# Squares, output weights and first feed-forward weights on GpSimd, and a linear layer inside the second mix

## What is computed

```python
x = _layernorm(x + L0_attn(x))   # differential attention, 16 heads of two score maps, full
x = _layernorm(x + L0_ffn(x))    # integer weights 2048 x 512, silu(g) * u
x = _layernorm(x + L1_attn(x))   # differential attention, causal, grouped keys and values
x = _layernorm(x + L1_ffn(x))    # x @ (weight * scale[:, None]).T + bias
# in both attentions, with attn1, attn2 = softmax(q k^T / 4) v of the two halves of a head:
attn = attn1 - lambda_full * attn2                             # 32 values a head
attn = attn * rsqrt(mean(attn * attn, -1) + 1e-5) * subln_w * (1.0 - LAMBDA_INIT)
out = attn.reshape(b, t, 512) @ wo.T
```

## Time and profile before

| | |
|---|---|
| three runs, us | 2482.46, 2478.36, 2482.72 (median 2482.46) |
| the profiled execution | 2479.18 us, span 2477.4 us |
| PE busy | 2344.1 us (95% of the span) |
| DVE busy | 1678.0 us (68%) |
| ACT busy | 1252.5 us (51%) |
| POOL busy | 190.1 us (8%) |
| phases, us from the start | L0 attention to 1021.2, mix0 to 1107.5, feed-forward to 1678.5, L1 attention to 2326.1, mix1 to 2412.7, linear to 2477.4 |

### The profile page before, as it was taken

The page is one execution under the profiler, slowest core; times in us unless marked ns, Lnnn a source line. Parts: engine busy times, 40 slices in busy tenths (PEclk is TensorE's granted clock), DMA queues, the critical chain, the costliest instruction groups (busy, mean ns, idle before and its releaser), DMA issues. The chain is left out here.

```text
span 2477.4 us, 43796 instructions
## 1 busy us (share of the span) xinstructions
PE 2344.1 (95%) x15600; PEld 1331.8 (54%) x15600; DVE 1678.0 (68%) x3848; ACT 1252.5 (51%) x2467; POOL 190.1 (8%) x341
## 2 busy tenths in 40 slices
PE   6999999999999999879999999967999999999877
PEld 5663333333333333458888888856644444444456
DVE  2357888888888887583344434452488888888586
ACT  2126666667666666652221121232266666666653
POOL 3000000000000000100000000000012211221103
PEclk9999999999999999999999999988899999999998
DMA  5664222232122200000000000003622222210001
GB/s 192 165 137 85 57 27 27 33 45 30 27 27 28 27 1 2 31 30 22 26 26 25 25 25 25 1 0 105 142 41 41 41 41 41 40 23 3 27 1 68
DMA packets 56684, 109.09 MB, mean 44 GB/s; under 512 B 11820, under 2 KB 22060, under 8 KB 56488
## 3 DMA queue, kind: packets, MB, share of 16 engines
q1 hardware_dynamic: 53960, 96.84, 19.7%
q0 software_dynamic: 2528, 9.70, 1.1%
HBM read 73.75 MB, written 31.46 MB: 42 GB/s over the span
## 5 line engine op out<-in xcount | busy, mean ns | idle before, releaser
L576 ACT ACTIVATE l_w_hi_prob<-l_p_work 128x512 f32<-128x512 f32 (+3 forms) x1792 | 871.0, 553 | 369.6 <-PE l_p_work L478 351.6
L628 DVE TENSOR_REDUCE l_maxima<-l_p_ring 128x1 f32<-128x512 f32 x1280 | 806.5, 684 | 134.8 <-PE l_p_ring L456 125.5
L498 PE MATMUL l_p_work<-l_w_hi_prob,v_all 128*32 128x512 f32 (+3 forms) x3584 | 806.6, 557 | 1.3 <-POOL l_w_hi_prob L432 0.9
L498 PE MATMUL l_p_work<-l_w_hi_prob,l_ones 128*32 128x512 f32 (+3 forms) x3584 | 806.3, 557 | 0.0
L478 PE MATMUL l_p_work<-xT_all 50*128 50x512 f32 (+3 forms) x1680 | 428.5, 409 | 0.0
L456 PE MATMUL l_p_ring<-xT_all 48*128 48x512 f32 (+3 forms) x1680 | 428.2, 412 | 0.0
L456 PEld LDWEIGHTS l_p_ring<-xT_all 48*128 48x128 f32 x1680 | 216.9, 185 | 233.2 <-DVE l_maxima L628 155.7
L498 PEld LDWEIGHTS l_p_work<-l_w_hi_prob,v_all 128*32 128x32 f32 x3584 | 166.7, 109 | 323.1 <-issue 197.7
L478 PEld LDWEIGHTS l_p_work<-xT_all 50*128 50x128 f32 x1680 | 222.1, 185 | 163.0 <-ACT l_w_hi_prob L576 113.3
L625 DVE CUSTOM_DVE_ANT_0 l_masked_scores<-l_p_ring,l_mask 128x128 bf16<-128x128 f32 (+3 forms) x512 | 239.4, 487 | 54.7 <-PE l_p_ring L456 44.8
L1098 DVE SCALAR_TENSOR_TENSOR ffn_h<-ffn_p_u,ffn_group_scales,ffn_silu 128x512 f32<-128x512 f32 x64 | 48.1, 751 | 211.9 <-PE ffn_p_u L226 205.9
(11 more groups left out here) (148 smaller groups left out, 2921.4 us busy)
## 6 DMA issues: line engine op xcount, KB each, us to landing
xT_all<-q_parts SPq DMA_DIRECT2D x180, 128.0 KB
q_parts<-l_part SPq DMA_DIRECT2D x64, 256.0 KB
xT_all<-k_parts SPq DMA_DIRECT2D x90, 128.0 KB
k_parts<-l_part SPq DMA_DIRECT2D x40, 256.0 KB
xT_all<-k_parts SPq DMA_DIRECT2D x90, 64.0 KB
x<-in_x_T SPq DMA_DIRECT2D x4, 1024.0 KB, 11.3
x<-in_L_attn_x POOLq DMA_DIRECT2D x1, 4096.0 KB, 16.0
out<-x SPq DMA_DIRECT2D x16, 256.0 KB, 2.0
```

Of the source, the lines that this page charges most:

```text
L498: summing = pe.matmul(p_out[r0:r0 + VD, off:CH], lhs, prob[step % PRING][:, sub, off:CH], start=first, stop=final)
L576: act.activation(prob[step % PRING][:, sub, off:CH], p_score[:, at % SCORE_BANKS, off:CH], ACT.Exp, scale=HD ** -0.5).then_inc(exped, 1)
L628: dve.tensor_reduce(to, scores, AX.X, ALU.max).then_inc(freed, 1)
```

## The change

- In both attention phases GpSimd squares each finished head (`square`): one multiplication and five additions that halve the columns, into a new tensor `mean_sq` of all tiles. It stands behind the masks of the following head; the last head's comes at the end of the phase.
- In heads 17 to 28 GpSimd also does one of 12 steps of scaling and splitting the output weights (`prepare_wo`).
- The mixes lose the preparation of the output weights and the stages for squares, mean squares, root and reciprocal; one root and one reciprocal of all tiles stand at the start. The multiplication of a tile moves to GpSimd. All lags become one shorter. Loads are issued on SP's queue.
- mix0 prepares the first feed-forward group whole on GpSimd, in 14 pieces between the tiles; `ffn_phase` starts with PE's products.
- `linear_phase` is gone. Its product, add, norm and store are stages of mix1, six and seven tiles behind; its weights are prepared on GpSimd in 12 steps during tiles 1 to 5, and the bias is added there once a tile has been turned.
- In the last feed-forward group each turn stands ahead of one down product (in the last chunk too, where it waits for the normalisation of the chunk before), and the rest of y ahead of each add; statistics come after the four adds, except in the last chunk; ScalarE's `y_value` comes before `deviation`.

```diff
@@ attention_phase, GpSimd @@
+            def square(n):
+                tiles = attn[:, :].rearrange("p (t c) -> p t c", c=D)
+                rows = slice((n // NH) * KT, (n // NH + 1) * KT)
+                head = tiles[:, rows, (n % NH) * VD:(n % NH + 1) * VD]
+                pool.wait_ge(out_kept, QC * (n + 1))
+                if n:
+                    pool.wait_ge(squared, HALVINGS * n)
+                pool.tensor_tensor(squares[:, :, :], head, head, ALU.mult).then_inc(squared, 1)
+                for i in range(1, HALVINGS):
+                    width = VD >> i
+                    to = squares[:, :, 0:width] if width > 1 else mean_sq[:, rows, n % NH:n % NH + 1]
+                    pool.wait_ge(squared, HALVINGS * n + i)
+                    pool.tensor_tensor(to, squares[:, :, 0:width], squares[:, :, width:2 * width], ALU.add
+                                       ).then_inc(squared, 1)
+            def prepare_wo(step):
+                k, what = divmod(step, 3)
...
+                if what == 0:
+                    op = pool.tensor_scalar(wo_stage[:, k, :], wo_stage[:, k, :], norm_w, 1.0 - LAMBDA_INIT, ALU.mult,
+                                            ALU.mult)
+                elif what == 1:
+                    op = pool.tensor_copy(wo_split.hi[:, k, :], wo_stage[:, k, :])
+                else:
+                    op = pool.tensor_tensor(wo_split.lo[:, k, :], wo_stage[:, k, :], wo_split.hi[:, k, :], ALU.subtract)
+                op.then_inc(wo_ready, 1)
             for n in range(HEADS):
                 for s in range(S):
                     if diagonal(s):
...
+                if n:
+                    square(n - 1)
+                if HEADS // 2 < n <= HEADS // 2 + 3 * KD:
+                    prepare_wo(n - HEADS // 2 - 1)
...
-            pool.wait_ge(loaded, 16 * len(loads))
+            square(HEADS - 1)
@@ mix_phase @@
+            def normalise_heads(t):
+                if t == 0:
+                    pool.wait_ge(inverted, 1)
+                if t >= 2:
+                    pool.wait_ge(turned, t - 1)
+                pool.tensor_tensor(normed[t % 2][:, :].rearrange("p (h w) -> p h w", w=VD),
+                                   attn[:, t * D:(t + 1) * D].rearrange("p (h w) -> p h w", w=VD),
+                                   inv_rms[:, t, :].unsqueeze(2).to_broadcast([P, NH, VD]), ALU.mult
+                                   ).then_inc(scaled, 1)
...
+            for t in range(NT + LAST_LAG):
+                if t < NT:
+                    normalise_heads(t)
+                if first and 2 <= t < NT:
+                    for i in range((t - 2) * pieces // (NT - 2), (t - 1) * pieces // (NT - 2)):
+                        prepare_first(i)
+                if last and 1 <= t <= LAST_LAG - 1:
+                    for i in range((t - 1) * 3 * KD // (LAST_LAG - 1), t * 3 * KD // (LAST_LAG - 1)):
+                        prepare_last(i)
+                if last and 0 <= t - LAST_LAG + 1 < NT:
+                    add_bias(t - LAST_LAG + 1)
...
-            tile_pipeline(dve, (1, invert), (4, scalars), (2, rest_of_turned), (6, rest_of_y), (0, mean_squares),
-                          (3, add))
+            dve.wait_ge(rooted, 1)
+            dve.reciprocal(inv_rms[:, :, :], inv_rms[:, :, :]).then_inc(inverted, 1)
+            later = ((LAST_LAG + 1, scalars(1)), (LAST_LAG, add(1))) if last else ()
+            tile_pipeline(dve, (3, scalars(0)), (1, rest_of_turned), (5, rest_of_y), (2, add(0)), *later,
+                          written_out=MIX_WRITTEN_OUT)
...
-            tile_pipeline(pe, (3, project), (5, turn_y), (1, turn), written_out=NT)
+            later = ((LAST_LAG, project_last),) if last else ()
+            tile_pipeline(pe, (2, project), (4, turn_y), (0, turn), *later, written_out=NT)
@@ ffn_phase, TensorE @@
-            def down(n, c, par, banks):
+            def down(n, c, par, banks, turned=None):
                 pe.wait_ge(h_lo, GT * n + GT)
                 for t in range(QPC):
+                    if turned is not None:
+                        turn(turned * QPC + t)
...
-            down(GROUPS * NCH - 1, NCH - 1, 1, 2)
-            turn(NCH - 2)
-            turn(NCH - 1)
+            down(GROUPS * NCH - 1, NCH - 1, 1, 2, NCH - 2)
+            for t in range(QPC):
+                turn((NCH - 1) * QPC + t)
```

More of the change, by code:

```diff
@@ L60 @@
 WRITTEN_OUT = 6
+LAST_LAG = 6
+HALVINGS = VD.bit_length()
+MIX_WRITTEN_OUT = 8
 GW = KD * GT * P
@@ L715, in tile_pipeline, with __init__, mix_phase @@
         step(i, i % 2, lambda t: t < NT)
-def mix_phase(nc, name, attn, wo_area, norm_w, x, xT, C, loads, convert=None):
+class FirstGroup:
+    def __init__(self, area, w, d_scale):
+        self.area, self.w, self.d_scale = area, w, d_scale
+class LastProduct:
+    def __init__(self, stage, w, scale, bias, out_d):
+        self.stage, self.w, self.scale, self.bias, self.out_d = stage, w, scale, bias, out_d
+def mix_phase(nc, name, attn, mean_sq, wo, x, xT, C, loads, first=None, last=None):
     with ExitStack() as ctx:
@@ L753, in mix_phase, with _ @@
         block = ctx.enter_context(nc.Block())
         tile = lambda t: x[:, ds(t, 1), :].squeeze(1)
+        @block.sync
+        def _(sp):
+            for dst, src in loads:
+                sp.dma_start(dst, src).then_inc(loaded, 16)
+            if last:
+                for t in range(NT):
+                    sp.wait_ge(y_done[1], t + 1)
+                    sp.dma_start(last.out_d[t * P:(t + 1) * P, :], x[:, t, :]).then_inc(stored, 16)
+                sp.wait_ge(stored, 16 * NT)
+            sp.wait_ge(loaded, 16 * len(loads))
@@ new lines, in prepare_last @@
+            def prepare_last(i):
+                what, k = divmod(i, KD)
+                if i == 0:
+                    pool.wait_ge(loaded, 16 * len(loads))
+                if i:
+                    pool.wait_ge(prepared, i)
+                if what == 0:
+                    op = pool.tensor_tensor(last.stage[:, k, :], last.stage[:, k, :], last.scale, ALU.mult)
+                elif what == 1:
+                    op = pool.tensor_copy(last.w.hi[:, k, :], last.stage[:, k, :])
+                else:
+                    op = pool.tensor_tensor(last.w.lo[:, k, :], last.stage[:, k, :], last.w.hi[:, k, :], ALU.subtract)
+                op.then_inc(prepared, 1)
@@ new lines, in add_bias @@
+            def add_bias(t):
+                pool.wait_ge(y_turned, t + 1)
+                pool.tensor_tensor(x[:, t, :], x[:, t, :], last.bias, ALU.add).then_inc(biased, 1)
+            pieces = (6 + GT + 3 * GW // CH) if first else 0
+            for t in range(NT + LAST_LAG):
[9 more added lines that the diff above has]
+                    add_bias(t - LAST_LAG + 1)
@@ L776, in scalars, with of @@
[L776 to L783, removed]
+            def scalars(l):
+                def of(t, par):
+                    dve.wait_ge(std_done[l], t + 1)
+                    wait_from_first(dve, y_done[l], t)
+                    dve.reciprocal(rstd[l][:, :], std[l][:, :]).then_inc(rstd_done[l], 1)
+                    dve.wait_ge(rstd_done[l], t + 1)
+                    dve.scalar_tensor_tensor(out=offset[l][:, :], in0=mv[l][:, 0:1], scalar=-1.0, in1=rstd[l][:, :],
+                                             op0=ALU.mult, op1=ALU.mult).then_inc(offset_done[l], 1)
+                return of
@@ L1272 @@
+            add(GROUPS * NCH - 1, NCH - 1, True, NCH - 2)
+            for t in range(QPC):
+                rest_of_y((NCH - 1) * QPC + t)
 class Constants:
```

373 lines of the change are left out of this document (154 added, 219 removed).

## The result

The changed kernel takes 2489.56 us (median of 7 runs, 2487.79 to 2496.92) against 2478.36 us for the kernel before, measured beside it: ratio 1.005, 95% interval 1.0033 to 1.0067. It is slower by 0.5%; forecast was 2473.8, faster. The profiled execution took 2488.43 us (span 2486.7; before 2477.4).

What follows compares the result with a forecast made beforehand. TensorE was taken as full nearly everywhere except the mixes, last feed-forward group and tail. Terms 2.6 - 5.1 - 7.0 - 12.6 + 0 + 40 - 26.6 = -8.7 us, from median 2482.46, gave 2473.8 us; range 2446 to 2504.

Steps and rivals of the forecast that it cites:

- Second attention: Heads of the second attention: GpSimd's squares and weights delay the next head's first mask, +40 us, bounds +10 and +79.
- What PE wins back: Second attention's head boundaries: PE recovers 0.6 us of a 1.6 us stall, leaving 1.0 us a head, 30 in all.
- rival A: Second attention's head boundaries: longer squares (3.0 us) and PE wins nothing back, +70 there, 2504 us in all; chance 0.24.
- The weights steps: Twelve heads of the second attention: output weights straight behind the squares, all on the path, 10 us.
- First mix, tiles: Tiles 0 to 15 of the first mix: 63.1 us against 68.2, -5.1 us, bounds -8.5 and +1.
- Start: Start of each mix: the new chain before the first product is longer, +1.4 us in the first, +1.2 in the second.
- entry: From first mix into feed-forward: first weights are prepared earlier on GpSimd, 0.3 us of 7.36 stays, -7.0 us.
- Last group: Last feed-forward group: turns dealt among down products, 70 us against 82.6, -12.6 us, bounds -8 and -16.
- Second mix and linear layer: Second mix with linear layer: PE sets 6.6 us a full step, 115 us against 141.6, -26.6 us, bounds 110 and 125.
- Heads of the first attention: First attention: GpSimd is idle there, its six operations a head cost 0 us, range 0 to +3.
- B: Second attention: the head boundary is nearly covered, squares 1.9 us, +16 there, 2450 us in all; chance 0.25.
- C: Both mixes: VectorE and GpSimd lock each other, +12 in the first, +8 in the second, 2494 us in all; chance 0.15.

Runs made afterwards that it cites:

- e4: Against e2, the multiplication that begins the squares runs twice in each head of the second attention: 2531.52 us, ratio 1.021 to the kernel before.
- e3: Against the changed kernel, only the squares move behind the fourth mask, the weights steps stay between the heads: 2416.89 us, ratio 0.9742 to the kernel before.
- e2: Against the changed kernel, only the 12 output weights steps move behind the fourth mask, the squares stay between heads: 2456.89 us, ratio 0.9907 to the kernel before.

## Why the prediction was wrong

**Second attention (+40 forecast, +72.9 measured): the step that failed.** Where the wait would come, on which queue and behind what, was right. So, nearly, was the length of the squares: 2.6 forecast, 2.4 measured. Two terms failed: 0.6 us a head that PE was to win back, where it won nothing, and a clock taken as full, where it fell.

- *What PE wins back.* I took a stall of 1.6 us and let PE win back 0.6, from the 1.0 us a head in which VectorE waited for PE. With squares of 2.4 us the same working gives a stall of 1.4, and the period grew by 1.41 (16.61 to 18.02): nothing came back, 30 x 1.41 = 42 instead of 30. That row was the wrong one for the purpose. It shows that VectorE runs ahead of PE; an engine that is busy for all of its time and then waits has no reserve to win back with. That was rival A's second condition.
- *The weights steps.* I took them at their own length, 10 us for twelve. They cost 30: 12 x (20.5 - 18.02). The own length was right as far as it goes: PE's waits in these heads are 26.1 us in sum, 10 more than 12 x 1.34. The other 20 are the clock, which was missing. Before, the clock was 1.00 over the whole stretch, and I carried that over, though I counted idle PE at the low clock in the last group. Behind the first 16 boundaries, with squares alone, it held (one wait of 2.27 us, then 15 of 1.34); in the twelve weights heads (waits of 1.91 to 2.57 us) it fell in eight; in e4 (nearly all 2.02 us) in 19 of 30. In e4 such a head cost 3.0 or 1.5 us more.

**First mix, tiles (-5.1 forecast, -12.2 measured).** PE was put at 3.89 us a tile and VectorE, with a charge for GpSimd's company, at 4.15. The tiles came every 3.69 us (12 of them in 44.3), PE busy for 43.8 us of 44.0 (1048 to 1092). That lies outside the bounds (3.9 to 4.6), so PE's own 3.89 was too high as well, and it makes about half of the 7.1 us missed. The other half is VectorE: 3.68 us was read from two starts in a stretch with waits, and 0.5 added to it, but VectorE's own work is 3.1 us a tile (36.4 us busy of the same 44.0), and GpSimd's company did not hold PE up. Start (+1.4, +1.2) and entry (-7.0, -7.1) were right; the last work of the mix and the first matmul stand like this (after; before, 7.36 us lay between the two):

```profile
1097.09 0.69 DVE L906 TENSOR_TENSOR xT_all<-mix_p_yT,xT_all 128x512 fp32r<-128x512 f32 x1 [0.20 <-ACT xT_all L956]
...
1098.11 1.19 PE L229 MATMUL ffn_p_g<-xT_all,first_hi 128*128 128x512 f32 x2 [1.68 <-PEq L779]
```

**Last group (-12.6, -13.7).** The order was right, and the idle PE stands where it was announced (5 to 6 us). The nearness of 70 to the measured 68.9 is luck: the terms written down (5.4, 10.7, 8.3, 10.7, 8.3, 5.8, four times 2.3, 3.7, 4.6) add up to 66.7. Up to turn 8 they give 49.2 us and the trace 49.1; from there to the first turn of the last chunk 12.9 and 13.1; turning back was put at 4.6 and took 6.7, at a mean clock of 0.51. Timeline, after, answering to the earlier trace rows:

```profile
1627.64 1.09 PE L1117 MATMUL ffn_p_d<-ident,x 128*128 128x128 f32 x4 [5.65 <-issue]
1628.38 0.78 PE L229 MATMUL ffn_p_d<-ffn_w_hi,attn_h_hi 128*128 128x512 f32 x1
...
1640.69 1.91 PE L1117 MATMUL ffn_p_d<-ident,x 128*128 128x128 f32 x8 [4.19 <-ACT x L1166]
```

**Second mix and linear layer (-26.6, -33.1).** 108.6 us lies outside the bounds of 110 and 125. A full step takes 6.35 us, not 6.6, and PE is busy in all of them, as forecast. The other terms erred to the same side: the first four tiles took 15.2 instead of 17.6, the tail with the last turns 17.7 instead of 18.3, and the extra microsecond for GpSimd's weights was not needed.

**Heads of the first attention (0, 0).** 26.20 us a head, 26.22 before. The 1.4 us in the table lies in the start; the runs here, with the same code in that stretch, scatter there by 3.5 us (1021.4 to 1024.9).

**The sum.** It is 18 us off, and the second attention alone 33: the mixes and the other stretches came out 15 us better than forecast and hid that much of the miss.

**Rivals.** A was right that nothing is won back. Its price of 70, against 73 measured, is luck: it had 60 for longer squares (3.0 us) and 10 for the weights, where 42 and 30 were measured, and it had no clock in it. Its 2504 came out too high because the rest gained 64 us rather than 49. B is out, PE won nothing back. C's lock exists, but its price in the mixes is zero: the offset operation took up to 916 ns beside GpSimd, and PE did not wait. VectorE's groups in the mixes (ns min/median/max, answering to the earlier trace rows):

```profile
L894 DVE SCALAR_TENSOR_TENSOR mix_offset<-mix_mv,mix_rstd x48: 158/160/916, 1039.9 to 2483.3; 128x1 f32<-128x1 f32 x48
```

## What to carry to other kernels

When work moves to an idle engine, look at what that engine's next urgent operation is and put the work behind it, where its queue waits longest: the same instructions cost 73 us between two heads and nothing in the middle of a head. Price a new wait of a saturated TensorE twice, once for its length and once for the stretch at 1.2 GHz that may follow; here the second was twice the first in the weights heads and two and a half times in e4. Read the slack from the moved work's own queue to the operation of the bound engine that waits for it, not from the gaps of the engines around it: in the earlier trace rows GpSimd is idle for 0.5 us before the first mask, and that mask ends 0.6 us before PE's sum, together the 1.0 or so that e3 shows as free.

## What the runs showed of the hardware

**The clock falls behind short waits.** In the heads of the second attention, 8 of 12 waits of 1.91 to 2.57 us in the kernel after and 19 of 30 in e4 (nearly all 2.02 us) were followed by a stretch at 1.2 GHz; none of the 16 waits of 1.34 us in the kernel after was, and none of the 28 of 1.33 us in e2. The length of the wait alone does not decide it: equal waits of 2.02 us went both ways from head to head (the rows of e4). What decides it stays open.

**VectorE waits out the rest of a GpSimd operation.** In e2 the subtraction of output weights begins just before VectorE's combination of halves, which reads two SBUF tensors (timelines of GpSimd and of VectorE):

```profile
2157.76 1.29 POOL L460 TENSOR_TENSOR wo_wo_lo<-wo,wo_hi 128x512 fp32r<-128x512 f32 x1
```

```profile
2158.03 1.16 DVE L709 SCALAR_TENSOR_TENSOR attn<-l_w_hi_half,neg_lambda 128x128 f32<-128x128 f32 x1
```

It takes 1.16 us instead of 0.35 and ends with the subtraction, and the head takes 0.4 us more. In the first attention one combination a head, which falls into the squares, went from 352 to some 574 ns, at no cost to the head's period. The Trainium skill (SBUF — State Buffer, section "SBUF: two separate sides") says that whichever of such a pair starts first has the shared ports for its whole instruction, and the other is blocked. By that rule, the trace agrees: when the combination started, 1.02 us were left of the subtraction's 1.29, and it took 1.16.

**GpSimd's short operations on two tensors** (groups, after): 612 ns for the multiplication of 256 columns and, for the additions,

```profile
L444 POOL TENSOR_TENSOR l_w_hi_squares<-l_w_hi_squares 128x128 f32<-128x128 f32 x64 | 29.4, 460 | 5.0
L444 POOL TENSOR_TENSOR l_w_hi_squares<-l_w_hi_squares 128x64 f32<-128x64 f32 x64 | 20.5, 321 | 5.0
L444 POOL TENSOR_TENSOR l_w_hi_squares<-l_w_hi_squares 128x32 f32<-128x32 f32 x64 | 16.2, 252 | 5.0
L444 POOL TENSOR_TENSOR l_w_hi_squares<-l_w_hi_squares 128x16 f32<-128x16 f32 x64 | 13.9, 217 | 5.0
L444 POOL TENSOR_TENSOR mean_sq<-l_w_hi_squares 128x8 f32<-128x8 f32 x64 | 13.3, 208 | 5.0
```

That is 0.18 us fixed and 2.2 ns a column, close to the line assumed (0.2 and 2.1). A multiplication of 512 columns in which one input is broadcast took 1.05 us instead of the 1.29 of the earlier trace rows. VectorE's reciprocal over 256 columns took 1.75 us (forecast 1.6).
